# Adding the first layer's expert outputs in smaller pieces and from an earlier row, and scattering the first half's rows earlier

## The chip, the cores and the metric

The kernel runs as one program on one core of a Trainium2 chip. The metric is the device time of one execution in microseconds, as the median of several runs. The core has five engines that run side by side and meet only at semaphores: TensorE (PE), VectorE (DVE), ScalarE (ACT), GpSimd (POOL) and SyncE (SP, which here only issues transfers). TensorE's weight loads are shown apart, as PEld.

## What is computed

Two layers over 4 x 1024 tokens of width 128. `attn0` is causal attention with rotated queries and keys, `conv1` a gated convolution of length 1024 done through Fourier transforms, `moe0` a mixture of 8 experts with one expert for each token, `moe1` one with two experts for each token.

```python
x = L0_attn_x                                   # 4 x 1024 x 128
xn = layernorm(x)
x = x + attn0(xn, w_q, w_k, w_v) + moe0(xn, wg, W, b)
xn = layernorm(x)
x = x + conv1(xn, Wu, Wv, W1, W2, W3, Wo, ...) + moe1(xn, Wg, W1, b1, W2, b2)
# moe1: p = softmax(xn @ Wg); the two best experts of each token;
#       y = (relu(xs @ W1[e] + b1[e]) @ W2[e] + b2[e]) * p, added at the token
```

## The kernel before

A tile is 128 tokens; there are 32 (`NT`), 8 for each batch entry (`J`). A quarter is 8 tiles, a half (`HT`) 16. The residual stays in SBUF as `xres`, and the normalised tokens in `row`.

The order on each engine is the order in which its block of the program is written, and there are three stages that matter here.

**The attention rows.** A loop `for n in range(NT)` runs on PE, DVE and ACT alike. In its turn n, TensorE multiplies the scores of row n+1 (`scores`), transposes the probabilities of row n once ACT has exponentiated them (`transpose_probs`, L1260), and weighs the values of row n-1 (`weigh_values`). DVE takes the maximum of row n+1 (`row_max`, L1710), copies a part of the transposed probabilities (`take_pt`) and adds the attention of row n-1 to `xres` (`attention_row`, L1728). ACT exponentiates row n+1 (`exp_rows`, L1008), which waits for that maximum. The scores of row n are n % 8 + 1 tiles wide, so that rows 24 to 27 are short and 28 to 31 long.

Into these turns other work is put by tables of turn numbers. `ADD_AT` (23, 24, 26) says in which turns DVE adds a quarter of the first layer's expert outputs (`add_experts`, L1744, then `tile_stats`, L1748, and `tile_aggr`, L1752); the fourth quarter follows in turns 28, 31 and behind the loop. The outputs are read back from memory (`moe0`) into the buffer `y0`, a quarter at a time, by SP (L731), and each load but the first waits until DVE has used the quarter before. POOL then computes the reciprocal deviations (`inverse_std`, L795 and L797). `NORM_AT` says when ACT normalises the first three quarters (L1025), `GATES_AT` (26, 27, 30) when TensorE transposes them and multiplies with the gate weights of the second layer, and ACT copies the logits to `lg`. `ROUTING_AT` spreads the 30 steps of the first half's routing (`routing1`, on DVE, L1510 to L1581) over turns 28, 29 and 30; `COUNTS_AT` (29) is the turn in which TensorE counts tokens for it.

**The prelude of the second layer.** POOL scatters the rows of the first half to the experts' slots in memory, one indirect transfer for each tile and each of the two chosen experts (`dispatch`, L810), 32 in all; behind every second one it waits until the transfers have been issued. It starts when `slot1_ready` says that the routing is done. TensorE meanwhile projects the tokens (`project_vu`, 16 units), transposes the last quarter, multiplies its gates and counts; DVE does the first radix passes (L622 and after) and the second half's routing; then TensorE does 8 Fourier products (`forward`), each followed by `product` on DVE (L1822 to L1827). The list is in `conv_at(PRELUDE)`. Behind the 32, POOL scatters 8 (`SCATTER_IN_PRELUDE`) of the second half's 32.

**The expert rounds.** There are 40 rounds, each for two tiles of slots. SP loads the slots (L710) once all 32 scatters of the first half have landed (`wait_sent1(0)`); TensorE transposes them (`expert_rows`, L1414) and multiplies twice, ACT copies the experts' weights into `ring` and takes the hidden layer, DVE adds a bias (`expert1_out`, L1873), POOL sends the rows back (`send_back`, L833). Convolution work for the second layer is spread over the same rounds, and two more of the second half's scatters follow in each round. `ring` is idle between the last tiles of the first layer's experts and the copies of the second layer's weights.

## Time and profile before

| | us |
|---|---|
| median of 3 runs | 510.49 (509.75 to 511.93) |
| the profiled execution, its own time | 510.97 |
| its span, first to last instruction | 509.2 |

| engine | busy us | share of the span |
|---|---|---|
| TensorE (PE) | 373.4 | 73% |
| PE weight loads | 305.5 | 60% |
| DVE | 294.5 | 58% |
| POOL | 256.7 | 50% |
| ACT | 225.5 | 44% |

The mean granted clock of TensorE over the span is 0.914 of full speed. A row of a timeline gives the start, the length, the engine, the line, the operation, what it writes and reads, how many instructions it groups, and in brackets how long the engine had been idle before it and which event ended that. No engine is busy all the time, so the busy shares alone do not say what bounds the kernel; the stretches and the waits at their ends do.

### The profile page before, as it was taken

To read this page: it belongs to the slowest core of one execution; us is meant where nothing else is said; L and a number is where in the kernel's file an instruction comes from. 1 tells how busy PE (TensorE), PEld (TensorE's weight loads), DVE (VectorE), ACT (ScalarE), POOL (GpSimd) and SP (SyncE) were. 2 spreads that over 40 slices of the span, in tenths; PEclk is the share of its full clock that TensorE was granted. 3 is DMA by queue.
4 is the path that set the end of the run, shared out by engine and by line. 5 is a ranking of instruction groups with operands and counts; after the bars stand their busy time and mean duration, and the time that the engine had idled before them with its cause. 6 is when DMAs were issued, how large, how long until landed. Compare 5 with 4: busy or idle time off the path is not lost.

```text
span 509.2 us, 7804 instructions
## 1 busy us (share of the span) xinstructions
PE 373.4 (73%) x2302; PEld 305.5 (60%) x2302; DVE 294.5 (58%) x782; ACT 225.5 (44%) x551; POOL 256.7 (50%) x254
## 2 busy tenths in 40 slices
PE   2483689979997954977997468888887777776630
PEld 0371255956784643757996357777776766766520
DVE  4968479216755776175769953367746773244115
ACT  1472042433342326252341036533557667578824
POOL 2746766615666013003766666666666445446540
PEclk9999699979998995696998859999999999999985
DMA  9999993632311112000113263444421213622407
GB/s 221 401 230 241 173 157 87 213 92 64 91 54 43 42 42 84 0 0 12 38 38 97 69 175 119 136 121 140 119 58 56 73 32 85 195 67 77 124 14 246
DMA packets 64745, 55.05 MB, mean 108 GB/s; under 512 B 6820, under 2 KB 56684, under 8 KB 64447
## 3 DMA queue, kind: packets, MB, share of 16 engines
q1 hardware_dynamic: 57888, 41.71, 33.0%
q0 software_dynamic: 6656, 12.51, 7.8%
q10 hardware_dynamic: 158, 0.33, 0.4%
q8 instruction: 19, 0.31, 0.3%
q14 instruction: 24, 0.19, 0.1%
HBM read 30.44 MB, written 25.27 MB: 109 GB/s over the span
## 4 chain that ended last, share of the span: by engine, by line
PE 39%; issue 16%; DMA 14%; ACT 12%; POOL 11%; DVE 7%; POOLq 1%; SPq 0%; ACTq 0%; DVEq 0%
PE psO L1158 15%; PE psS L1158 14%; PE psT L1158 7%; ACT hT L1120 7%; DMA slots<-row,slot 7%; POOL slots L823 4%; POOL slots L810 3%; POOL w L844 2%; DMA moe<-ys,xs 2%; DMA xres<-in_x 2%; PE psT L1260 2%; ACT row L1025 1%; POOL moe L833 1%; DVE xres L1744 1%; DVE work L1710 1%
## 5 line engine op out<-in xcount | busy, mean ns | idle before, releaser
L833 POOL DMA_INDIRECT moe<-ys,xs x61 | 62.8, 1029 | 61.4 <-DVE ys L1873 23.4
L810 POOL DMA_INDIRECT slots<-row,slot x64 | 67.1, 1048 | 35.7 <-DMA slots<-row,slot 12.3
L1158 PE MATMUL psO<-ring,hT 128*128 128x128 f32 x320 | 46.1, 288 | 44.2 <-ACT hT L1120 44.2
L1158 PEld LDWEIGHTS psO<-ring,hT 128*128 128x128 f32 x320 | 39.5, 194 | 52.6 <-issue 52.6
L1873 DVE TENSOR_TENSOR ys<-psO,ring 128x256 f32<-128x256 f32 x40 | 16.9, 424 | 85.9 <-PE psO L1158 85.7
L1120 ACT ACTIVATE hT<-psT,ring 128x128 f32<-128x128 f32 x160 | 45.6, 368 | 46.0 <-PE psT L1158 45.8
L1053 ACT ACTIVATE ring<-w 128x642 f32 x80 | 55.7, 761 | 0.9 <-issue 0.8
L1158 PE MATMUL psS<-work 128*128 128x512 f32 (+3 forms) x96 | 41.4, 545 | 12.3 <-DVE work L1693 8.8
L833 POOL DMA_INDIRECT moe<-ys,w x35 | 37.1, 1060 | 23.8 <-DVE ys L1873 9.7
L1018 ACT ACTIVATE work<-psT 128x512 f32<-128x512 f32 (+3 forms) x32 | 16.5, 517 | 66.2 <-PE psT L1260 66.2
L823 POOL DMA_INDIRECT slots<-row,slot x32 | 34.7, 1085 | 18.2 <-DMA slots<-row,slot 10.9
L1158 PE MATMUL psT<-xsT,ring 128*128 128x128 f32 x320 | 43.3, 279 | 0.5 <-ACT xsT L1113 0.5
L1158 PEld LDWEIGHTS psT<-xsT,ring 128*128 128x128 f32 x320 | 40.7, 195 | 1.4 <-ACT xsT L1113 0.8
L1158 PE MATMUL psO<-work 128*128 128x128 f32 x288 | 41.3, 294 | 0.0
L1008 ACT ACTIVATE work<-psS,work 128x128 f32<-128x128 f32 (+7 forms) x32 | 23.6, 739 | 38.9 <-DVE work L1714 38.8
L1710 DVE TENSOR_REDUCE work<-psS 128x1 f32<-128x128 f32 (+7 forms) x32 | 24.0, 749 | 26.0 <-PE psS L1158 24.5
L1158 PEld LDWEIGHTS psO<-work 128*128 128x128 f32 x288 | 38.8, 211 | 0.0
L795 POOL TENSOR_SCALAR veps<-mv 128x8 f32<-128x8 f32 (+1 forms) x9 | 2.4, 265 | 68.4 <-DVE slot L1577 32.6
L1260 PE MATMUL psT<-cst,work 128*128 128x128 f32 x144 | 24.6, 304 | 13.8 <-ACT work L1008 13.8
L1158 PEld LDWEIGHTS psS<-work 128*128 128x128 f32 x96 | 18.0, 214 | 27.0 <-issue 18.6
L1158 PE MATMUL psS<-work,mats 128*128 128x256 f32 x128 | 32.0, 411 | 2.9 <-DVE work L673 2.6
L1158 PE MATMUL psS<-xT,work 128*128 128x512 f32 x64 | 30.9, 625 | 1.3 <-ACT work L1008 1.3
(271 smaller groups left out, 801.1 us busy)
## 6 DMA issues: line engine op xcount, KB each, us to landing
slots<-xs SPq DMA_DIRECT2D x14, 516.0 KB, 12.7
mats<-in_iv SPq DMA_DIRECT2D x16, 256.0 KB, 3.4
xs<-slots SPq DMA_DIRECT2D x61, 64.5 KB, 1.9
w<-in_w SPq DMA_DIRECT2D x8, 321.0 KB
w<-slots SPq DMA_DIRECT2D x35, 64.5 KB, 1.9
xres<-in_x SPq DMA_DIRECT2D x4, 512.0 KB, 9.5
mats<-in_fw SPq DMA_DIRECT2D x1, 2048.0 KB, 11.1
moe<-xs SPq DMA_DIRECT2D x4, 512.0 KB, 6.9
```

Source lines behind the costliest of these rows:

```text
L810: pool.indirect_dma_start(slots1[:, :], bass.IndirectOffsetOnAxis(ap=(slot1, slot2)[k][:, i:i + 1], axis=0), row[:, i, :], None, bounds_ch ...
L823: pool.indirect_dma_start(dst[:, :], bass.IndirectOffsetOnAxis(ap=slots[:, i:i + 1], axis=0), row[:, i, :], None, bounds_check=bound, oob_ ...
L833: pool.indirect_dma_start(dst[:, :], bass.IndirectOffsetOnAxis(ap=row_slots[l][m][:, D:ROWW].bitcast(I32), axis=0), ys[:, n % UNROLL, :], ...
L844: pool.tensor_tensor(t[0:FO, :], t[0:FO, :], hx[0:FO, :], op).then_inc(f_pool, 1)
L1008: act.activation(prob[n % 2][:, 0:(i + 1) * P], S[n % 2][:, :, :].rearrange("p a m -> p (a m)")[:, 0:(i + 1) * P], ACT.Exp, bias=negmax[:, ...
L1018: act.activation(pT[n % 2][:, 0:k, :].rearrange("p j q -> p (j q)"), t_bank("p", n, 0)[:, 0:k * P], ACT.Copy).then_inc(pt_act, 1)
L1053: act.activation(pair_w[p % RING_PAIRS][:, t, :], w12[:, bass.ds(e, 1), :].rearrange("p e h -> p (e h)"), ACT.Copy).then_inc(e_w, 1)
L1120: last = act.activation(hT[:, k, :], TP[1][:, k * P:(k + 1) * P], ACT.Relu, bias=pair_w[p % RING_PAIRS][:, k // 2, B1_AT + k % 2:B1_AT + k ...
L1158: return pe.matmul(o, lhsT, rhs, start=start, stop=stop)
L1260: last = pe.transpose(t_bank("p", n, c)[:, (j - 4 * c) * P:(j - 4 * c + 1) * P], prob[n % 2][:, j * P:(j + 1) * P], ident)
L1710: dve.tensor_reduce(negmax[:, n:n + 1], S[n % 2][:, :, :].rearrange("p a m -> p (a m)")[:, 0:(n % J + 1) * P], X, ALU.max, negate=True).th ...
L1873: tt(ys[:, m:m + 2, :], O[p % 2][:, 0:2 * D].rearrange("p (t d) -> p t d", d=D), pair_w[p % RING_PAIRS][:, :, B2_AT:W_COLS], ALU.add).then ...
```

## The change

Four things are changed together.

- The loads of the expert outputs: quarters 0, 1 and 2 go to three buffers (`y0` and two parts of `ring`) and are issued one behind the other; quarter 3 waits for the use of quarter 0. Each has a semaphore of its own. ACT waits for the use of the first three before it copies weights into `ring`.
- The additions: pieces of four tiles (later two and one), each with its statistics, some before the row maximum of a turn (`ADD_BEFORE_MAX`) and some behind the row (`ADD_BEHIND_ROW`), from turn 21 on.
- Norms, gates and counts are two turns earlier or so, and the routing of the first half is in turns 26 to 28, again partly before the row maximum.
- In the prelude, the last quarter's transposes and gates come behind 5 and 8 projections, not 8 and 10; both halves of the last quarter's `inverse_std` stand inside the scatter (before dispatch 4 and 12); 12 of the second half's scatters are done ahead of the rounds, not 8; and SP loads the first inverse matrices behind slots 3, 5 and 14, not four of them ahead of all slots.

`ISSUES_APART_IN_ROUNDS` is 2, as `ISSUES_APART` is, and changes nothing.

```diff
-GATES_AT = (26, 27, 30)
-NORM_AT = {25: [(0, 0), (0, 1)], 26: [(1, 0), (1, 1)], 28: [(2, 0)], 29: [(2, 1)]}
-ROUTING_AT = {28: 12, 29: 10, 30: R1_STEPS}
-COUNTS_AT = 29
+GATES_AT = (24, 25, 29)
+NORM_AT = {23: [(0, 0), (0, 1)], 24: [(1, 0), (1, 1)], 27: [(2, 0)], 28: [(2, 1)]}
+COUNTS_AT = 27
-ADD_AT = (23, 24, 26)
+ADD_BEFORE_MAX = {22: (4, 8), 23: (12, 16), 25: (20, 24), 29: (24, 28), 31: (28, 30)}
+ADD_BEHIND_ROW = {21: (0, 4), 22: (8, 12), 24: (16, 20)}
+ROUTING_BEFORE_MAX = {26: 6, 28: 8}
+ROUTING_BEHIND_ROW = {26: 6, 27: 10, 28: R1_STEPS}
-SCATTER_IN_PRELUDE, SCATTER_PIECES = 8, 2
-NORM_IN_SCATTER = 6
+SCATTER_IN_PRELUDE, SCATTER_PIECES = 12, 2
+NORM_IN_SCATTER = (4, 12)
+FIRST_INV_MATS = {3: (0, 1), 5: (2, 3), 14: (4, 5, 6, 7)}
-        return (vu[:8] + [("t", 2 * B - 2), ("t", 2 * B - 1)] + vu[8:10] + [("g", B - 1)] + vu[10:14] + [("rc", 2)] + vu[14:]
+        return (vu[:5] + [("t", 2 * B - 2), ("t", 2 * B - 1)] + vu[5:8] + [("g", B - 1)] + vu[8:12] + [("rc", 2)] + vu[12:]
+        y0_groups = [y0, *(ring[:, n * J * D:(n + 1) * J * D].rearrange("p (j d) -> p j d", d=D) for n in range(2)), y0]
             for g in range(B):
-                if g:
-                    sp.wait_ge(y0_used, J * g)
-                sp.dma_start(y0, moe0[g * L:(g + 1) * L, :].rearrange("(j p) d -> p j d", p=P)).then_inc(y0_loaded, 16)
+                if g == B - 1:
+                    sp.wait_ge(y0_used, J)
+                sp.dma_start(y0_groups[g], moe0[g * L:(g + 1) * L, :].rearrange("(j p) d -> p j d", p=P)).then_inc(y0_loaded[g], 16)
-            for c in range(NC // 2):
-                inverse_mats(0, c)
             wait_sent1(0)
...
-                if n == RING[1] - 1:
-                    for c in range(NC // 2, NC):
+                if n in FIRST_INV_MATS:
+                    for c in FIRST_INV_MATS[n]:
                         inverse_mats(0, c)
...
-            inverse_std(2 * B - 1, 0, J // 2)
             for i in range(HT):
-                if i == NORM_IN_SCATTER:
-                    inverse_std(2 * B - 1, J // 2, J // 2)
+                if i in NORM_IN_SCATTER:
+                    inverse_std(2 * B - 1, J // 2 * NORM_IN_SCATTER.index(i), J // 2)
                 dispatch(0, 0, i)
...
+            act.wait_ge(y0_used, (B - 1) * J)
...
+            def add_tiles(first, end):
+                for stage in (add_experts, tile_stats, tile_aggr):
+                    for i in range(first, end):
+                        stage(i)
...
+                if n in ADD_BEFORE_MAX:
+                    add_tiles(*ADD_BEFORE_MAX[n])
+                take(first_routing, ROUTING_BEFORE_MAX.get(n, 0))
                 if n + 1 < NT:
                     row_max(n + 1)
```

The DVE order at turns 23 and 24 before: L1710 and L1714 are the maximum of row 24, L1767 the reciprocal sum, L1722 the copy of probabilities, L1728 the attention's addition, and the eight tiles follow.

```order
208 L1710 TENSOR_REDUCE work<-psS 128x1
209 L1714 TENSOR_SCALAR work<-work 128x1
210 L1767 RECIPROCAL work<-work 128x1
211 L1722 COPY work<-psT 128x512
212 L1728 SCALAR_TENSOR_TENSOR xres<-psO,work,xres 128x128
213 L1744 SCALAR_TENSOR_TENSOR xres<-work,gate,xres 128x128 x8
214 L1748 BN_STATS stats<-xres 128x6 x8
215 L1752 BN_AGGR mv<-stats 128x2 x8
216 L1710 TENSOR_REDUCE work<-psS 128x1
```

The DVE order now, in turns 22 and 23: L1713 is the row maximum (row 23, then row 24), L1747 the addition; the third and fourth piece read from `ring`.

```order
206 L1747 SCALAR_TENSOR_TENSOR xres<-work,gate,xres 128x128 x4
207 L1751 BN_STATS stats<-xres 128x6 x4
208 L1755 BN_AGGR mv<-stats 128x2 x4
209 L1713 TENSOR_REDUCE work<-psS 128x1
210 L1717 TENSOR_SCALAR work<-work 128x1
211 L1778 RECIPROCAL work<-work 128x1
212 L1725 COPY work<-psT 128x384
213 L1731 SCALAR_TENSOR_TENSOR xres<-psO,work,xres 128x128
214 L1747 SCALAR_TENSOR_TENSOR xres<-ring,gate,xres 128x128 x4
```

By the maximum of row 24, 16 tiles have been added where none had been.

POOL before, from the last quarter's first deviations (L795, L797) through the scatters (L810) to the first rows sent back (L833).

```order
40 L795 TENSOR_SCALAR veps<-mv 128x4
41 L797 TENSOR_TENSOR rstd<-veps,cst 128x4
42 L810 DMA slots<-row,slot 10240x129 x6
43 L795 TENSOR_SCALAR veps<-mv 128x4
44 L797 TENSOR_TENSOR rstd<-veps,cst 128x4
45 L810 DMA slots<-row,slot 10240x129 x10
46 L819 COPY row<-cst 128x8 x2
47 L810 DMA slots<-row,slot 10240x129 x24
48 L833 DMA moe<-ys,xs 8192x128 x2
```

POOL now, the same place (L813 is the scatter, L798 and L800 the deviations, L836 the sending back).

```order
40 L813 DMA slots<-row,slot 10240x129 x4
41 L798 TENSOR_SCALAR veps<-mv 128x4
42 L800 TENSOR_TENSOR rstd<-veps,cst 128x4
43 L813 DMA slots<-row,slot 10240x129 x8
44 L798 TENSOR_SCALAR veps<-mv 128x4
45 L800 TENSOR_TENSOR rstd<-veps,cst 128x4
46 L813 DMA slots<-row,slot 10240x129 x4
47 L822 COPY row<-cst 128x8 x2
48 L813 DMA slots<-row,slot 10240x129 x28
49 L836 DMA moe<-ys,xs 8192x128 x2
```

Four scatters now stand ahead of the first deviations and twelve ahead of the second; 28, not 24, stand between the relabelling (`second_ids`) and the first sending back.

SP before, from the loads of the expert outputs on.

```order
23 L731 DMA work<-moe 128x8x128 x4
24 L738 DMA mats<-in_iv 128x512 x4
25 L710 DMA xs<-slots 128x129 x8
26 L710 DMA w<-slots 128x129 x7
27 L738 DMA mats<-in_iv 128x512 x4
```

SP now.

```order
23 L736 DMA work<-moe 128x8x128
24 L736 DMA ring<-moe 128x8x128 x2
25 L736 DMA work<-moe 128x8x128
26 L715 DMA xs<-slots 128x129 x4
27 L743 DMA mats<-in_iv 128x512 x2
28 L715 DMA xs<-slots 128x129 x2
29 L743 DMA mats<-in_iv 128x512 x2
```

The first inverse matrices moved behind the first four slot loads.

## Rows read from the trace of the kernel before

**Rows 1.** Busy time of each engine in stretches: microseconds, instructions, granted clock, DMA.

```profile
core 0: us, PE busy (x) PEld busy (x) DVE busy (x) ACT busy (x) POOL busy (x), PEclk, DMA share, GB/s
168.29:243.53 75.24, 56.11 (x300) 45.34 (x301) 45.52 (x178) 27.68 (x68) 12.44 (x19) 0.80 0.10 30
243.53:270.38 26.85, 24.24 (x220) 23.33 (x217) 19.50 (x52) 12.62 (x23) 18.07 (x19) 1.00 0.11 36
270.38:286.67 16.29, 16.01 (x64) 13.12 (x64) 14.84 (x39) 0.00 (x0) 10.15 (x11) 0.90 0.38 105
286.67:296.22 9.55, 0.00 (x1) 0.01 (x1) 8.82 (x17) 0.00 (x0) 6.31 (x7) 0.61 0.21 59
296.22:311.17 14.95, 12.48 (x55) 10.66 (x56) 4.10 (x9) 8.14 (x19) 10.02 (x10) 0.68 0.66 177
```

**Rows 2.** Timeline of TensorE: prelude's start, Fourier products, first slots of the rounds.

```profile
243.53 0.22 PE L1158 MATMUL psS<-biasb,pickb 96*128 96x128 bf16 x1
...
270.38 14.04 PE L1158 MATMUL psS<-work,mats 128*128 128x256 f32 x56 [2.61 <-DVE work L673]
...
296.22 0.74 PE L1414 MATMUL psT<-cst,xs 128*128 128x128 f32 x2 [9.55 <-DMA xs<-slots]
...
297.43 2.08 PE L1158 MATMUL psT<-xsT,ring 128*128 128x128 f32 x8 [0.47 <-ACT xsT L1113]
```

**Rows 3.** Timeline of POOL's scatter and of SP's first slot loads.

```profile
235.68 0.23 POOL L795 TENSOR_SCALAR veps<-mv 128x4 f32<-128x4 f32 x1 [32.62 <-DVE slot L1577]
...
243.47 0.97 POOL L810 DMA_INDIRECT slots<-row,slot  x1 [0.78 <-DMA slots<-row,slot]
...
250.89 2.02 POOL L810 DMA_INDIRECT slots<-row,slot  x1 [0.78 <-DMA slots<-row,slot]
...
290.74 0.97 POOL L810 DMA_INDIRECT slots<-row,slot  x1 [0.30 <-issue]
...
294.00 3.66 SPq L710 DMA_DIRECT2D xs<-slots  x8
```

**Rows 4.** Timeline of DVE in the attention rows: additions, routing, last statistics.

```profile
176.43 1.22 DVE L1710 TENSOR_REDUCE work<-psS 128x1 f32<-128x1024 f32 x1
...
182.09 2.18 DVE L1744 SCALAR_TENSOR_TENSOR xres<-work,gate,xres 128x128 f32<-128x128 f32 x8
...
185.75 0.62 DVE L1752 BATCH_NORM_AGGREGATE mv<-stats 128x2 f32<-128x6 f32 x8
...
218.05 0.36 DVE L1510 TENSOR_REDUCE m<-lg 128x16 f32<-128x128 f32 x1
...
235.24 0.17 DVE L1577 CAST slot<-m 128x16 int32<-128x16 f32 x1
...
245.52 0.36 DVE L1752 BATCH_NORM_AGGREGATE mv<-stats 128x2 f32<-128x6 f32 x4
```

**Rows 5.** TensorE's waits for the exponentials, 168.3 to 243.5 us, grouped.

```profile
L1260 PE MATMUL psT<-cst,work 128*128 128x128 f32 x57 | 10.6, 330 | 10.6 <-ACT work L1008 10.6
```

**Rows 6.** Timeline: ACT's norms of one quarter, and the first gates on TensorE.

```profile
193.74 3.17 ACT L1025 ACTIVATE row<-xres,veps,rstd 128x128 f32<-128x128 f32 x8
...
201.65 3.55 PE L1158 MATMUL psO<-wg,xT 128*128 128x8 f32 x16 [3.20 <-ACT xT L1030]
```

**Rows 7.** SP's first load of expert outputs, and the four from issue to landing.

```profile
166.02 0.37 SPq L731 DMA_DIRECT2D work<-moe  x1
...
work<-moe SPq DMA_DIRECT2D x4, 512.0 KB, 3.9
```

**Rows 8.** Timeline of DVE: second routing's wait, the first three rounds' outputs.

```profile
259.97 0.37 DVE L1510 TENSOR_REDUCE m<-lg 128x16 f32<-128x128 f32 x1 [4.16 <-ACT lg L1034]
...
302.91 0.42 DVE L1873 TENSOR_TENSOR ys<-psO,ring 128x256 f32<-128x256 f32 x1 [5.61 <-PE psO L1158]
...
311.20 0.42 DVE L1873 TENSOR_TENSOR ys<-psO,ring 128x256 f32<-128x256 f32 x1 [5.28 <-PE psO L1158]
...
318.00 0.42 DVE L1873 TENSOR_TENSOR ys<-psO,ring 128x256 f32<-128x256 f32 x1 [3.37 <-PE psO L1158]
```

More of the change, by code:

```diff
@@ L228 @@
 ISSUES_APART = 2
+ISSUES_APART_IN_ROUNDS = 2
 def conv_at(r):
@@ L491, in two_layer_kernel @@
         e_ha = sem("e_ha")
-        y0_loaded = sem("y0_loaded")
+        y0_loaded = [sem(f"y0_loaded{g}") for g in range(B)]
         y0_used = sem("y0_used")
@@ L799, in _, with after_issue @@
             n_issued = [0]
-            def after_issue():
+            def after_issue(apart=ISSUES_APART):
                 n_issued[0] += 1
-                if n_issued[0] % ISSUES_APART == 0:
+                if n_issued[0] % apart == 0:
                     pool.wait_ge(issued, n_issued[0])
@@ L836, in send_back @@
                     engine_sem=issued).then_inc(sent_back[m], 16)
-                after_issue()
+                after_issue(ISSUES_APART_IN_ROUNDS if l else ISSUES_APART)
             n_pool = [0]
@@ L1741, in add_experts @@
                 g, j = divmod(i, J)
[L1742 removed]
+                dve.wait_ge(y0_loaded[g], 16)
                 dve.wait_ge(o_done, i + 1)
[L1744 removed]
+                stt(xres[:, i, :], y0_groups[g][:, j, :], gate0[:, i:i + 1], xres[:, i, :], ALU.mult, ALU.add).then_inc(y0_used, 1)
             def tile_stats(i):
@@ L1780, in _ @@
                     expert0_bias(e)
-                if n in ADD_AT:
-                    g = ADD_AT.index(n)
-                    for stage in (add_experts, tile_stats, tile_aggr):
-                        for i in range(J * g, J * g + J):
-                            stage(i)
-                if n in ROUTING_AT:
-                    take(first_routing, ROUTING_AT[n])
-                if n == NT - 4:
-                    for stage in (add_experts, tile_stats):
-                        for i in range(NT - 8, NT - 4):
-                            stage(i)
-                if n == NT - 3:
-                    for i in range(NT - 8, NT - 4):
-                        tile_aggr(i)
+                if n in ADD_BEHIND_ROW:
+                    add_tiles(*ADD_BEHIND_ROW[n])
+                take(first_routing, ROUTING_BEHIND_ROW.get(n, 0))
                 if n == NT - 1:
                     norm_rows(2 * B - 1, 0, J // 2)
-                    for i in range(NT - 4, NT - 1):
-                        add_experts(i)
+                    add_tiles(NT - 2, NT - 1)
             attention_row(NT - 1)
-            add_experts(NT - 1)
-            for stage in (tile_stats, tile_aggr):
-                for i in range(NT - 4, NT):
-                    stage(i)
+            add_tiles(NT - 1, NT)
             norm_rows(2 * B - 1, J // 2, J // 2)
```

4 lines of the change are left out of this document (1 added, 3 removed).

## The prediction

> **What bounds the kernel now.** I read the stretches first [rows 1], then TensorE's waits [rows 2, 5], then the engines that end them. The rounds start only when TensorE has the first slots: it finishes its Fourier products at 286.67 and stands still for 9.55 us, until the loads that SP issued at 294.00 land [rows 2, 3]. Those loads wait for POOL's 32 scatters. POOL begins at 235.68, at once when DVE has written the slot numbers, and the last of the 32 is issued at 290.74 [rows 3]. So the chain before the rounds is: routing done on DVE, then 294.00 - 235.68 = 58.32 us of scatter, then 2.22 us of load. Beside it runs a second chain that is 9.55 us shorter: attention rows end at 243.53, 26.85 us of projections, 16.29 us of Fourier products [rows 1, 2]. From the rounds on nothing of the order changes much, so whatever the start gains, the end gains; the reader should see that two chains have to be shortened together, and that the shorter one caps the gain.
>
> The stage that feeds both is the attention rows from turn 21 on: 75.24 us with TensorE busy for 56.11 at a clock of 0.80 [rows 1]. Of its 19.1 us idle, 10.6 are waits for an exponential [rows 5], and those wait for a row maximum that stands behind added work in DVE's queue.
>
> **The additions (turns 21 to 25).** The sum over eight tiles was 182.09 to 186.37, 4.28 us [rows 4], so a piece of four is about 2.1 us. Nothing is added or removed in all: about 17 us of DVE work moves to other places, and DVE is busy for only 45.5 of the 75.2 us [rows 1]. The first load is issued at 166.02 and lands 3.9 us later, at 169.9 [rows 7], in time for turn 21 at about 171. The next two go into other buffers; even one behind the other at 3.9 us each they land by 177.8, before their use at about 181 and 189. A cost lies in turns 21 and 22: two pieces, 4.3 us, stand ahead of the maximum of row 23, which was at 176.43 [rows 4]; about 1.6 us of it fill time in which DVE waited for the projections there, so the maximum comes at about 179.1, and TensorE loses 2.7 us. After that the same work is no longer in turns 23 and 24. By my hand schedule, with these lengths and the waits of each engine's order: 16 tiles are added by 186, where before eight had been at 186.37, and the second eight followed at about 192.5. I take 6.5 us sooner for the second quarter.
>
> **Norms, gates and routing.** ACT needs 3.17 us for a quarter, and the first gates take 3.55 us at the low clock [rows 6]. From 186 on: deviations, about 2.7 us; the first quarter's norms are done at about 190.5, the second's at 194.6; the first gates run from 195 to 199, row 26's scores and the second transposes follow, and the second gates' logits are there at about 205.4. Routing's first step was at 218.05 and slots were written at 235.41 [rows 4], 17.4 us for 28 steps with row work between. Now its first 6 steps stand before the maximum of row 27, and wait for those logits: 205.4. The 28 steps are some 10 us of DVE; between them stand three row maxima and their small work (4 us) and ACT's exponential. I get the slots at about 219.5. The bounds are 218 (no low clock in the gates) and 226 (every wait before a maximum costs TensorE a full round trip again). So POOL starts 16.2 us sooner (9.7 to 17.7).
>
> TensorE pays for it: it stands idle while the maximum of row 29 waits behind 8 steps of routing, about 5 us, where it now idles before rows 30 and 31. The end of the rows comes from that: with the clock of before I get 242, with full clock 239, and no gain at all is 243.53. I take 242, 1.5 us sooner, since the gaps are as many as before and the clock of 0.80 is the nearest row.
>
> **The scatter.** It starts at 219.5. Its 58.32 us hold both pairs of deviations, and so they do now. New is a wait before dispatch 12: POOL gets there some 20 us after its start, at 240, but the last tile's statistics come about 1.3 us behind the rows' end (2.35 us before, for four tiles [rows 4]), at 243.3, so 3 us are lost. Slots are loaded from 219.5 + 58.3 + 3 = 280.8, and TensorE has them at 283.0.
>
> A scatter instruction takes 0.97 us, but 2.02 at 250.89, where DVE runs its 128x1024 additions; the one at 243.47, under the expert additions, takes 0.97 [rows 3]. Of the Trainium skill, "SBUF — State Buffer", section "SBUF: two separate sides", speaks against this change here: DVE instructions with two SBUF inputs and GpSimd instructions that read SBUF shut each other out for a whole instruction. By it, the 12 scatters that now run beside the rows' additions could each be held up for one of them, 0.28 us; the row at 243.47 doesn't show it. I leave it at nothing in the sum; by the rule, the first slots would come at up to 286.4.
>
> **The prelude.** The last quarter's gates stand two projections earlier, and DVE waited 4.16 us for them [rows 8]. Of 26.85 us for 16 projections and the rest, one is some 1.35 us, so the second routing starts 2.7 us sooner and the Fourier products too; TensorE waited 2.61 us for that radix pass [rows 2], which bounds this gain. TensorE is done at 242 + 24.1 + 16.3 = 282.4. Both chains thus meet at 282 to 283. The 12 scatters, 4 more than before, put 6 us ahead of the first sending back; DVE needs the buffers of rounds 0 and 1 only four rounds later, 27 us, which hides them. The matrices that SP loads behind slots 3 and 5 are needed two hand-offs later and were loaded early before; at most 1 us.
>
> **The clock.** TensorE enters the rounds at a clock of 0.61 to 0.68 after its 9.55 us of idleness [rows 1]; its first 8 multiplications take 2.08 us, and the first two outputs are 8.29 us apart, the next two 6.80 [rows 8]. With an idle time under 1 us that penalty mostly goes: 1.5 us for the first round, about 1 us for each of two groups of eight. I take 3 us; the ends are 0 and 4.
>
> **The sum.** 296.22 - 283.0 = 13.2 us, and 3 for the clock: 16.2. The profiled execution's 510.97 becomes 494.8; the median of the runs is 0.5 below it, so I say 495.0 for both.
>
> **Rivals.**
> 1. *The routing comes late.* DVE's queue waits for the second quarter's logits before the maximum of row 27, and so TensorE, ACT and DVE take turns. For it: three engines' hand-offs lie between norms and logits. Slots at 226 give first slots at 289.5, a gain of 6.7 and some 2 of clock: 502 (499 to 505).
> 2. *DVE bounds the first rounds.* Its products end some 18 us behind the routing, at about 290.5, and three radix pieces stand ahead of the first output, which so comes at 294 and not at 289. Against it: rounds need that output only two rounds later. If it stops ACT's third weight copy, 3 us are lost: 498.
> 3. *The rows gain more.* Rows end at 239, POOL starts at 218, and the clock is full: first slots at 279.5 to 281, 4 of clock: 487 to 491.
> 4. *Slower.* The pieces before a maximum each hold up exponential, transposes and the next scores, five of them 2.1 us and two of routing 2 to 2.6, some 15 us in all, and none is paid back by the waits that go. It decides once the rows end more than 12.3 us later (9.55 of slack and 2.7 of the prelude), at 256 or more, which also delays the last quarter's norms inside POOL's queue: 511 to 517, say 514. Against it: DVE's work there is the same as before and it idles 30 us.
>
> **Chances.** The forecast (491 to 499) 0.52; rival 1 0.20; rival 2 0.07; rival 3 0.11; slower 0.07; within 0.5% (the parts cancel) 0.03. 0.5%, 2.6 us, is about what a measurement of this kernel can tell from no change. The range 489 to 503 leaves out rival 4, no change, and the far ends of rivals 1 and 3, 0.19 in all. Faster: 0.90.
>
> **What would show it.** Right: POOL's scatter starts at 218 to 221; the maximum of row 23 is 2 to 3 us late; TensorE's wait before the first slots falls from 9.55 us to under 2; the clock of the first round is above 0.9, and its outputs are 6.8 us apart; the rounds after it last as long as before. Wrong: the first scatter at 226 or later; an idle time of over 4 us at the first slots (the scatter alone bounds); a wait of DVE for sent rows in round 4 (the 12 scatters cost something); rows ending later than 246.

## The result, and the profile of the changed kernel

The changed kernel takes **492.23 us** (median of 4 runs, 491.0 to 493.85); the kernel before took 510.73 in the runs beside it. The ratio is 0.9639, with an interval of 0.9600 to 0.9677: faster by 3.6%. The profiled execution took 493.04, its span 491.2, at a mean granted clock of 0.934 (0.914 before). The forecast of 495.0 was 2.8 us too high.

In short: POOL's scatter starts 17 us sooner and the step in it that wants the last tile holds it up for only 2.9 us, the attention rows end 5 us sooner, so the first slots are transposed 15 us sooner; another 3 us come from a TensorE that no longer enters the rounds at its low clock.

The times inside the changed kernel's trace are read with one correction. Upstream of anything that the change touches its timeline is already about 1.0 us late (the maximum of row 22 stands at 169.25, before at 168.29 in [rows 1]), so a milestone that moved by x gained about x + 1. That lateness is a difference between executions: in a second trace of the same kernel (changed_again) the maximum of row 22 stands at 166.64. The third output and the span are compared as they stand.

First the stretches, at the same events as [rows 1] (columns as there: length of the stretch, busy time and instructions of each engine, granted clock, DMA); the last two lines divide the rounds at the second output.

```profile
169.25:238.19 68.94, 52.57 (x300) 41.12 (x301) 46.15 (x183) 27.98 (x68) 20.40 (x26) 0.85 0.14 40
238.19:265.57 27.38, 24.25 (x220) 23.35 (x218) 21.73 (x57) 10.62 (x20) 16.86 (x17) 1.00 0.09 30
265.57:281.08 15.51, 15.51 (x67) 13.30 (x65) 13.57 (x32) 2.08 (x3) 9.70 (x11) 0.89 0.19 51
281.08:293.11 12.03, 8.64 (x56) 7.54 (x55) 11.26 (x23) 8.06 (x19) 8.49 (x7) 1.00 0.95 276
293.11:318.00 24.89, 21.58 (x128) 19.10 (x126) 11.05 (x22) 11.94 (x29) 15.96 (x18) 1.00 0.36 106
```

Read the first number behind the colon pairs against [rows 1]: rows 75.24 to 68.94, prelude 26.85 to 27.38, Fourier products 16.29 to 15.51, and the stretch of 9.55 us in which TensorE waited for slots is not there at all. The first slots come at 281.08 and not at 296.22.

TensorE's timeline has the same events (start, length, engine, line, operation, how many, and in brackets the idle time ahead and what ended it), and two waits that matter.

```profile
220.91 1.54 PE L1263 MATMUL psT<-cst,work 128*128 128x128 f32 x6 [6.54 <-ACT work L1010]
...
227.73 3.33 PE L1161 MATMUL psS<-work 128*128 128x512 f32 x4
...
238.19 0.22 PE L1161 MATMUL psS<-biasb,pickb 96*128 96x128 bf16 x1
...
264.23 0.23 PE L1161 MATMUL psS<-biasb,pickb 96*128 96x128 bf16 x1 [3.13 <-DVE tables L1530]
...
265.57 15.67 PE L1161 MATMUL psS<-work,mats 128*128 128x256 f32 x64
281.08 0.40 PE L1417 MATMUL psT<-cst,xs 128*128 128x128 f32 x2
281.95 1.16 PE L1161 MATMUL psT<-xsT,ring 128*128 128x128 f32 x8 [0.47 <-ACT xsT L1115]
```

Against [rows 2]: the brackets at the first slots are gone, and the first eight multiplications take 1.16 us where they took 2.08. The wait of 2.61 us before the Fourier products is gone too, but one of 3.13 us ends 1.3 us ahead of them: TensorE wants to write a bank of PSUM that DVE's routing (L1530) has not read yet.

POOL and SP, to set against [rows 3]:

```profile
218.78 1.12 POOL L813 DMA_INDIRECT slots<-row,slot  x1 [22.37 <-DVE slot L1580]
220.20 0.97 POOL L813 DMA_INDIRECT slots<-row,slot  x1 [0.30 <-issue]
...
240.27 0.23 POOL L798 TENSOR_SCALAR veps<-mv 128x4 f32<-128x4 f32 x1 [2.87 <-DVE mv L1755]
...
260.63 2.52 POOL L813 DMA_INDIRECT slots<-row,slot  x1 [0.89 <-DMA slots<-row,slot]
```

```profile
278.53 1.80 SPq L715 DMA_DIRECT2D xs<-slots  x4
```

The scatter starts at 218.78, waits 2.87 us for the last statistics before dispatch 12, and lets SP load at 278.53, 15.5 us sooner than the 294.00 of before. With 2.2 us to land that is 280.7: the slots are there just before TensorE is. Both chains now meet, and TensorE's is the last by a few tenths of a microsecond.

DVE, to set against [rows 4] and [rows 8]:

```profile
179.60 1.19 DVE L1713 TENSOR_REDUCE work<-psS 128x1 f32<-128x1024 f32 x1
...
185.59 0.36 DVE L1755 BATCH_NORM_AGGREGATE mv<-stats 128x2 f32<-128x6 f32 x4
...
204.08 0.37 DVE L1513 TENSOR_REDUCE m<-lg 128x16 f32<-128x128 f32 x1 [3.50 <-ACT lg L1036]
...
217.71 0.17 DVE L1580 CAST slot<-m 128x16 int32<-128x16 f32 x1
...
289.89 0.42 DVE L1868 TENSOR_TENSOR ys<-psO,ring 128x256 f32<-128x256 f32 x1
293.11 0.42 DVE L1868 TENSOR_TENSOR ys<-psO,ring 128x256 f32<-128x256 f32 x1 [0.25 <-PE psO L1161]
299.91 0.42 DVE L1868 TENSOR_TENSOR ys<-psO,ring 128x256 f32<-128x256 f32 x1 [3.37 <-PE psO L1161]
```

The maximum of row 23 is 3.2 us later than the 176.43 of before (2.2 with the correction), the 16th tile's statistics are there at 185.95, the routing begins 14 us sooner and the slot numbers are written 17.5 us sooner. The third output is 18.1 us sooner (318.00 to 299.91) and the span 18.0 us shorter (509.2 to 491.2): nothing behind the third output changed.

### The profile page after: what moved, and what is told of

Read it like the earlier page. It is cut to its first block, busy times and chain, and to the rows that moved or that the text cites. A ratio compares the mean times of both kernels' runs of the same rounds, so it can differ in the third digit from the quotient of the medians.

```text
span 491.2 us, 7805 instructions
## 1 busy us (share of the span) xinstructions
PE 366.0 (75%) x2302; PEld 298.7 (61%) x2302; DVE 294.4 (60%) x782; ACT 225.9 (46%) x551; POOL 258.4 (53%) x254
## 4 chain that ended last, share of the span: by engine, by line
PE 44%; issue 13%; ACT 12%; DVE 10%; DMA 10%; POOL 8%; SPq 1%; ACTq 0%; POOLq 0%; DVEq 0%
PE psS L1161 19%; PE psO L1161 15%; PE psT L1161 7%; ACT hT L1122 7%; POOL slots L826 4%; DMA slots<-row,slot 4%; DMA moe<-ys,xs 2%; POOL w L847 2%; DMA xres<-in_x 2%; ACT row L1027 1%; PE psT L1263 1%; POOL moe L836 1%; DVE work L1713 1%; DVE xres L1747 1%; DMA moe<-ys,ring 1%
## 5 line engine op out<-in xcount | busy, mean ns | idle before, releaser
L813 POOL DMA_INDIRECT slots<-row,slot x64 | 69.3, 1083 | 57.0 <-DVE slot L1580 22.4
L836 POOL DMA_INDIRECT moe<-ys,xs x61 | 61.1, 1001 | 58.3 <-issue 16.6
L1161 PE MATMUL psS<-work 128*128 128x512 f32 (+3 forms) x96 | 42.6, 558 | 12.6 <-DVE work L1696 8.8
L836 POOL DMA_INDIRECT moe<-ys,w x35 | 38.0, 1087 | 23.3 <-DVE ys L1868 9.7
L826 POOL DMA_INDIRECT slots<-row,slot x32 | 34.9, 1091 | 18.1 <-DMA slots<-row,slot 10.9
L1161 PE MATMUL psT<-xsT,ring 128*128 128x128 f32 x320 | 42.3, 275 | 0.5 <-ACT xsT L1115 0.5
L1161 PE MATMUL psO<-work 128*128 128x128 f32 x288 | 39.7, 286 | 0.0
L1713 DVE TENSOR_REDUCE work<-psS 128x1 f32<-128x128 f32 (+7 forms) x32 | 24.0, 750 | 25.5 <-PE psS L1161 23.9
L1161 PEld LDWEIGHTS psO<-work 128*128 128x128 f32 x288 | 37.1, 203 | 0.0
L1161 PEld LDWEIGHTS psS<-work 128*128 128x128 f32 x96 | 17.9, 214 | 27.5 <-issue 18.5
L1263 PEld LDWEIGHTS psT<-cst,work 128*128 128x128 f32 x144 | 17.0, 153 | 23.2 <-ACT work L1010 18.3
L1161 PE MATMUL psS<-work,mats 128*128 128x256 f32 x128 | 30.1, 395 | 0.0
```

The lines of the kernel that those rows point to most:

```text
L813: pool.indirect_dma_start(slots1[:, :], bass.IndirectOffsetOnAxis(ap=(slot1, slot2)[k][:, i:i + 1], axis=0), row[:, i, :], None, bounds_ch ...
L826: pool.indirect_dma_start(dst[:, :], bass.IndirectOffsetOnAxis(ap=slots[:, i:i + 1], axis=0), row[:, i, :], None, bounds_check=bound, oob_ ...
L836: pool.indirect_dma_start(dst[:, :], bass.IndirectOffsetOnAxis(ap=row_slots[l][m][:, D:ROWW].bitcast(I32), axis=0), ys[:, n % UNROLL, :], ...
L1161: return pe.matmul(o, lhsT, rhs, start=start, stop=stop)
L1263: last = pe.transpose(t_bank("p", n, c)[:, (j - 4 * c) * P:(j - 4 * c + 1) * P], prob[n % 2][:, j * P:(j + 1) * P], ident)
L1713: dve.tensor_reduce(negmax[:, n:n + 1], S[n % 2][:, :, :].rearrange("p a m -> p (a m)")[:, 0:(n % J + 1) * P], X, ALU.max, negate=True).th ...
```

## Experiments

Each kernel ran beside the kernel before on its own chip. Medians are compared through those runs; milestones are from the traces. "The changed kernel with ..." names what is edited in it.

**One part undone.** Four kernels ran together (the kernel before beside them: 512.1).

The order of the prelude as before:

```diff
-        return (vu[:5] + [("t", 2 * B - 2), ("t", 2 * B - 1)] + vu[5:8] + [("g", B - 1)] + vu[8:12] + [("rc", 2)] + vu[12:]
+        return (vu[:8] + [("t", 2 * B - 2), ("t", 2 * B - 1)] + vu[8:10] + [("g", B - 1)] + vu[10:14] + [("rc", 2)] + vu[14:]
```

> The changed kernel, with only the order of the prelude put back (8 projections ahead of the last quarter's transposes, 10 ahead of its gates, 14 ahead of the counts). Theory of the prediction (the earlier gates bring the Fourier products 2.7 us sooner, and these lead to the first round): 2.7 us longer than the changed kernel, near 495. Rival, from the trace of the changed kernel: there TensorE waits 3.13 us for routing results in the bank of the counts, which took the gain back, so this kernel starts its Fourier products 0 to 0.5 us apart from the changed one and takes the same time, within 0.7 us; DVE's products end some 2 us later, which the first two rounds hide.

493.71 us, ratio 0.9662 (0.9618 to 0.9707). TensorE's timeline:

```profile
264.56 14.12 PE L1161 MATMUL psS<-work,mats 128*128 128x256 f32 x56 [2.59 <-DVE work L678]
```

The rows end at 237.72, so the Fourier products start 26.84 us behind them, as before the change (26.85), and with the change they start 27.38 us behind. The gates really come sooner, but the counts also do: they stand behind 12 projections, not 14, hold a PSUM bank until DVE has reached L1530, and a projection that rotates onto that bank waits for it. One wait was exchanged for another. By the ratios this kernel is 1.2 us longer than the changed one, which the intervals don't tell apart; the 2.7 us of the theory are not there.

The deviations of the last quarter where they were, the first before all scatters, the second before dispatch 6:

```diff
-NORM_IN_SCATTER = (4, 12)
+NORM_IN_SCATTER = 6
...
+            inverse_std(2 * B - 1, 0, J // 2)
             for i in range(HT):
-                if i in NORM_IN_SCATTER:
-                    inverse_std(2 * B - 1, J // 2 * NORM_IN_SCATTER.index(i), J // 2)
+                if i == NORM_IN_SCATTER:
+                    inverse_std(2 * B - 1, J // 2, J // 2)
```

> The changed kernel, with only the places of the last quarter's deviations in POOL's scatter put back (first pair ahead of all scatters, second behind 6). Theory (the scatter chain leads to the first round, and the places keep POOL from waiting for the end of the attention rows): the scatter starts at 223.8 and not 218.8, six scatters are done by the wait for the last tile at 240 where it was twelve, so the first slots come 9 us later and the kernel takes 500 to 502. Rival (Fourier products lead, the scatter has slack): under 3 us longer.

505.0 us, ratio 0.9878 (0.9834 to 0.9922). POOL's two deviations, and TensorE's first slots:

```profile
223.90 0.23 POOL L798 TENSOR_SCALAR veps<-mv 128x4 f32<-128x4 f32 x1 [28.32 <-DVE mv L1756]
...
241.41 0.23 POOL L798 TENSOR_SCALAR veps<-mv 128x4 f32<-128x4 f32 x1 [7.49 <-DVE mv L1756]
```

```profile
290.90 0.47 PE L1418 MATMUL psT<-cst,xs 128*128 128x128 f32 x1 [8.49 <-DMA xs<-slots]
```

With the slot numbers there at 219.07, about as in the changed kernel, POOL stands 4.8 us before its first scatter, since the first pair of deviations wants tiles 24 to 27, and 7.49 us before its seventh, since the second wants the last tile. SP loads at 289.14, 10.6 us later; TensorE's idle time comes back, and with it the low clock (0.50 from 290.90 to 298.38), so that the third output stands 22.53 us behind the first slots and not 18.83. The expectation of 500 to 502 had left that out. The third output is 13.5 us later (313.43), but some 2 us of it aren't the edit's: this execution was the longest of its four, its second gates took 3.56 us and not 1.92, and its rows end 2.0 us later behind the maximum of row 23. By the ratios of the runs (0.9878 and 0.9639) this one edit carries some 12 of the 18.5 us.

It can do so only together with the rows. In the kernel before there is no such wait to take away; POOL stands there for 0.35 us:

```profile
246.07 0.23 POOL L795 TENSOR_SCALAR veps<-mv 128x4 f32<-128x4 f32 x1 [0.35 <-DVE mv L1752]
```

No run has the new places without the new rows.

The loads into one buffer, one behind the use of the other:

```diff
-        y0_groups = [y0, *(ring[:, n * J * D:(n + 1) * J * D].rearrange("p (j d) -> p j d", d=D) for n in range(2)), y0]
+        y0_groups = [y0, y0, y0, y0]
...
-                if g == B - 1:
-                    sp.wait_ge(y0_used, J)
+                if g:
+                    sp.wait_ge(y0_used, J * g)
```

> The changed kernel with one buffer for the expert outputs, each load behind the use of the quarter before. Theory: the pieces leave time for a load of 3.9 us, DVE waits some 0.9 us in turn 22 and 0.5 us in turn 24, routing and rows come about 1 us later: 492 to 494. Rival (three loads at once are what lets the additions start in turn 21): 4 us or more longer, 496 and up.

494.22 us, ratio 0.9669 (0.9635 to 0.9702); third output at 300.33, 0.4 us later; by the ratios 1.5 us longer, with intervals that overlap. The early pieces hardly need the three buffers: a load of 3.9 us finds its place between two quarters.

8 scatters in the prelude and the inverse matrices first:

```diff
-SCATTER_IN_PRELUDE, SCATTER_PIECES = 12, 2
+SCATTER_IN_PRELUDE, SCATTER_PIECES = 8, 2
-FIRST_INV_MATS = {3: (0, 1), 5: (2, 3), 14: (4, 5, 6, 7)}
+FIRST_INV_MATS = {14: (4, 5, 6, 7)}
...
+            for c in range(NC // 2):
+                inverse_mats(0, c)
             wait_sent1(0)
```

> The changed kernel with 8 scatters of the second half ahead of the rounds and the first four inverse matrices loaded ahead of all slots. Theory: both are hidden before and after, 491.5 to 493, the same as the changed kernel. Rival (12 scatters shorten the rounds, or the matrices delayed the first inverse products): over 1.5 us apart.

495.41 us, ratio 0.9696 (0.9653 to 0.9740); third output at 300.73. POOL sends the first rows back at 290.80, not at 299.32, and it brings nothing, since DVE needs the buffers only rounds later. The third output is 0.8 us later than in the changed kernel: the first slots come 0.9 us sooner (280.18), and the first round, where this execution had a low clock, gives up 1.7 (eight output products 2.05 us, 1.13 in the changed kernel). The expectation of 491.5 to 493 was missed. By the ratios this kernel is 2.9 us longer, with intervals that overlap, and the trace is that of its shortest execution. So whether the two edits are worth anything is open.

**One part alone**, and two questions on waits (the kernel before beside them: 510.51). The attention rows, loads and routing of the change, with the prelude's order, the deviations, the 8 scatters and the matrices of before:

```diff
-SCATTER_IN_PRELUDE, SCATTER_PIECES = 12, 2
-NORM_IN_SCATTER = (4, 12)
-FIRST_INV_MATS = {3: (0, 1), 5: (2, 3), 14: (4, 5, 6, 7)}
+SCATTER_IN_PRELUDE, SCATTER_PIECES = 8, 2
+NORM_IN_SCATTER = 6
+FIRST_INV_MATS = {14: (4, 5, 6, 7)}
...
-        return (vu[:5] + [("t", 2 * B - 2), ("t", 2 * B - 1)] + vu[5:8] + [("g", B - 1)] + vu[8:12] + [("rc", 2)] + vu[12:]
+        return (vu[:8] + [("t", 2 * B - 2), ("t", 2 * B - 1)] + vu[8:10] + [("g", B - 1)] + vu[10:14] + [("rc", 2)] + vu[14:]
```

> The kernel before with only the attention rows changed (additions in pieces, three loads, earlier norms, gates and routing); prelude order, deviations' places, 8 scatters and matrices as before. Theory (scatter chain, which loses 9 us to the old places of the deviations): 500 to 502, about half of the gain. Rival (the rows bring the gain, the rest is small): 493 to 495.

504.3 us, ratio 0.9873 (0.9825 to 0.9921), 2 to 4 us more than expected, and again the low clock had been left out (first slots to third output 21.85 us, 18.83 in the changed kernel). The rows end as early as in the changed kernel (237.25), and the gain stays unused:

```profile
289.78 1.09 PE L1420 MATMUL psT<-cst,xs 128*128 128x128 f32 x2 [9.40 <-DMA xs<-slots]
```

Rows alone bring 6.2 us. No run has the rows and the places of the deviations alone; that these two bring most of the 18.5 follows from undo_norm_places and from the runs with another part undone, which lose 1.2 to 2.9 us each by the ratios.

The kernel before with the prelude's order, the 12 scatters and the matrices of the change:

```diff
-SCATTER_IN_PRELUDE, SCATTER_PIECES = 8, 2
+SCATTER_IN_PRELUDE, SCATTER_PIECES = 12, 2
+FIRST_INV_MATS = {3: (0, 1), 5: (2, 3), 14: (4, 5, 6, 7)}
...
-        return (vu[:8] + [("t", 2 * B - 2), ("t", 2 * B - 1)] + vu[8:10] + [("g", B - 1)] + vu[10:14] + [("rc", 2)] + vu[14:]
+        return (vu[:5] + [("t", 2 * B - 2), ("t", 2 * B - 1)] + vu[5:8] + [("g", B - 1)] + vu[8:12] + [("rc", 2)] + vu[12:]
```

> The kernel before with only the prelude's order, 12 scatters and the matrices' places changed. Theory: the Fourier products were 9.55 us ahead of the first slots, so nothing that moves them counts: 510 to 511.5. Rival (the parts add up, 2.7 us of the prelude): 508.

511.38 us, ratio 1.0007 (0.9980 to 1.0033): nothing, with the same 3.13 us of wait for L1526 and one of 8.11 before the first slots. The second would have hidden a gain as well as a loss, so this run shows the wait for the bank and not the worth of the order.

The kernel before, with TensorE kept busy while it waits for the first slots, by 150 small multiplications whose result nothing uses:

```diff
+                if r + 2 == 0:
+                    for _ in range(150):
+                        mm(TP[1][:, 0:P], identb[:, :], onesb[:, :])
                 if 0 <= r + 2 < PAIRS1:
                     expert_rows(r + 2)
```

> The kernel before with 150 small multiplications of TensorE into an unused bank between the Fourier products and the first slots, about 8 us of work in a wait of 9.55 us; their result is used by nothing. Theory (the idle time lowers the clock for the first round, 3 us): first slots at the same time, the first two outputs of DVE 6.8 and not 8.3 us apart, 507 to 508.5. Rival (the low clock in the first round costs nothing on the chain, or has another cause than idleness): 510 to 511.

508.61 us, ratio 0.9958 (0.9930 to 0.9986). TensorE's timeline:

```profile
287.54 8.54 PE L1158 MATMUL psT<-onesb,identb 128*128 128x128 bf16 x150
297.05 0.69 PE L1414 MATMUL psT<-cst,xs 128*128 128x128 f32 x2 [0.97 <-DMA xs<-slots]
298.21 1.16 PE L1158 MATMUL psT<-xsT,ring 128*128 128x128 f32 x8 [0.47 <-ACT xsT L1113]
```

The slots come no sooner, yet the first eight multiplications take 1.16 us and not 2.08, and the outputs stand at 302.40, 309.20 and 316.00: 6.80 apart, not 8.29 and 6.80 as in [rows 8]. That isolates the clock's part: 1.9 us by the medians, 2.8 by the traces (first slots to third output 18.95 us, 21.78 before). So about 2 to 3 us of the gain come from TensorE not standing still before the rounds, whatever ends its wait. The Trainium skill, "TensorE: Matmul & The Clock Gate", section "HAM oscillation — how this bites in real kernels", tells of idle time that puts the array back to its lower clock, the time being lost afterwards; this pair of runs agrees.

All of the third part of the routing behind row 28 instead of 8 steps ahead of the maximum of row 29:

```diff
-ROUTING_BEFORE_MAX = {26: 6, 28: 8}
+ROUTING_BEFORE_MAX = {26: 6}
```

> The changed kernel with the last 8 routing steps behind the row of turn 28 and not ahead of the maximum of row 29. TensorE's wait of 6.54 us there shrinks by 2.6, so the rows end that much sooner; the scatter starts 1.8 us later. Theory A (the scatter waits for the end of the rows before dispatch 12, so the rows' end leads and not its start): 1 to 2 us shorter than the changed kernel, 490 to 491.5. Theory B (the start of the scatter leads): 1.8 us longer, 494.

496.09 us, ratio 0.9703 (0.9651 to 0.9755). TensorE's wait before row 29's transposes halves, and another opens:

```profile
219.10 1.26 PE L1263 MATMUL psT<-cst,work 128*128 128x128 f32 x6 [3.38 <-ACT work L1010]
...
225.49 0.66 PE L1281 MATMUL psT<-cst,row 128*128 128x128 f32 x4 [2.33 <-DVE work L1725]
```

I had expected the rows to end 2.6 us sooner; they end at 240.68, 2.5 later, and the scatter starts 2.8 later. The steps stand in DVE's queue ahead of the maximum of row 30 instead, and the 3.16 us that the first wait lost come back as 2.33 in the other. The rest of the lateness isn't the edit's: the routing's first step, which comes before it, is already 1.0 us late (205.08), and the second and third gates took 3.56 us each and not 1.92. So this place was no better, and by how much it is worse is not shown.

**Towards a better version** (the kernel before beside the first three: 509.75, beside the last: 511.25). The changed kernel once more, for a reference on the same chip:

> The changed kernel itself, once more, as the measure for the kernels beside it on the same chip: 491 to 494.

492.22 us, ratio 0.9659 (0.9621 to 0.9697); the same rows as in the first trace, among them the 3.13 us and a wait of POOL of 2.80. One row is new: though the maximum of row 22 is 2.6 us sooner here (166.64), that of row 23 is only 1.1 sooner (178.51), because DVE waits 1.42 us for the first load of expert outputs before its first addition (170.71). The additions now begin so early that the load can hold them up, which it could not before the change.

The last deviations before dispatch 14, and the counts behind 14 projections, where the bank is no longer in the way:

```diff
-NORM_IN_SCATTER = (4, 12)
+NORM_IN_SCATTER = (4, 14)
-vu[8:12] + [("rc", 2)] + vu[12:]
+vu[8:14] + [("rc", 2)] + vu[14:]
```

> The changed kernel with the last tile's deviations before dispatch 14 and not 12, and the second half's counts behind 14 projections and not 12. Theory (three chains end together at the first slots: the scatter with its wait of 2.87 us at dispatch 12, the Fourier products with TensorE's wait of 3.13 us for the counts' bank, and neither alone can give more than the other): both waits go, TensorE has the first slots 2.5 us sooner, DVE's products end 0.6 us sooner, 2 to 2.6 us shorter than the changed kernel. Rival (DVE's products and radix pieces ahead of the first output lead by now): 0.6 us shorter at most.

491.93 us, ratio 0.9641 (0.9597 to 0.9684): no gain that can be told. Both waits are gone, and the first slots come 40.5 us behind the rows' end, not 42.9; but the third output only 60.8 behind it, not 61.7. The scatter is no longer what leads: SP loads at 273.91, 4.3 us ahead of TensorE's first slots (278.25). TensorE then runs at a low clock in the first round, in this stretch and these two groups:

```profile
282.00:289.00 7.00, 6.85 (x31) 6.21 (x32) 6.69 (x12) 2.70 (x6) 4.84 (x5) 0.76 0.97 273
...
282.15 1.95 PE L1161 MATMUL psO<-ring,hT 128*128 128x128 f32 x8 [1.66 <-issue]
283.89 4.50 PE L1161 MATMUL psS<-work,mats 128*128 128x256 f32 x16
```

The two groups take 1.13 and 3.62 us in the changed kernel; the 1.7 us between are about what the first round lost (20.33 us from the first slots to the third output, 18.83 in the changed kernel). The rival, that DVE's products lead by now, doesn't explain it: busy_before_row_29 below has the same prelude and the same work on DVE, and there it is 18.66. Why the clock fell is open. TensorE had stood still for 1.66 us just before, but it does so at the same place in the changed kernel too (1.81 us), and there the clock held.

The same counts with the deviations of the changed kernel, 50 multiplications that nothing uses before the first gates, and 100 before row 28's transposes:

```diff
-vu[8:12] + [("rc", 2)] + vu[12:]
+vu[8:14] + [("rc", 2)] + vu[14:]
+                    if g == 0:
+                        for _ in range(50):
+                            mm(o_bank("g", g)[:, 0:P], identb[:, :], onesb[:, :])
...
+                if n == 28:
+                    wait_emptied(pe, T_USES, T_AT[("p", n, 0)])
+                    for _ in range(100):
+                        mm(t_bank("p", n, 0)[:, 0:P], identb[:, :], onesb[:, :])
```

> The changed kernel with the counts behind 14 projections, and 50 small unused multiplications of TensorE in its wait before the first gates (3.4 us) and 100 in its wait of turn 28 (6.5 us). Theory (the clock falls in those waits, and the slow multiplications behind them stand on the chain): gates take 1.9 and not 3.55 us, scores of row 31 1.9 and not 3.3, the rows end 3 us sooner, POOL no longer waits at dispatch 12; first slots 4 to 5 us sooner, 487 to 489. Rival (the slow multiplications lie beside waits for other engines): within 1 us of the changed kernel.

491.23 us, ratio 0.9622 (0.9586 to 0.9659). The expectation of 487 to 489 was missed. The profiled execution was the longest of its six (495.5), so its third output (302.15) says little. The first gates take 1.92 us and not 3.55, and with both traces lined up at their start the routing's first step is 2.0 us sooner, but the rows' end only 0.7, as the third gates took 3.22 us here and not 1.92. POOL waits 4.26 us before dispatch 12 and TensorE 2.04 us for the slots, so with the deviations there the scatter leads again. And I had put the 100 one row too early: the 6.54 us of wait are before row 29's transposes. So the last run has them there, and the deviations before dispatch 14:

```diff
-NORM_IN_SCATTER = (4, 12)
+NORM_IN_SCATTER = (4, 14)
-                if n == 28:
+                if n == 29:
```

> The changed kernel with four edits: the last norm before dispatch 14 instead of 12, the counts behind 14 projections instead of 12, 50 multiplications whose result nothing uses ahead of the first gates, and 100 of them ahead of row 29's transposes, in the 6.55 us in which TensorE waits for that exponential. Theory that the clock falls after that wait and that this sets the rows' end: gates(0) at 1.9 us, the scores behind row 29's transposes at about 1.95 us instead of 3.3, the gates of the third quarter at 1.9, rows' end 2 us sooner (235.1 to 236 on the changed kernel's timeline of 237.1 to 238.2), Fourier products start 25.5 us behind it, first scatter about 1.5 us sooner, no wait of POOL for the last statistics; third output at 296 to 297 instead of 298.8 to 299.9; median 488.5 to 490. Rival, that the row maxima and exponentials and not TensorE's clock set the rows' end: fillers take as long as the wait at most, rows end within 0.5 us of before, third output at 298 to 299.5, median 491 to 492.5. The 100 take 5.8 us at full clock, more at the low one: should they end behind the exponential, the rows are up to 3 us later, median 493 to 495.

**489.55 us** (487.42 to 493.49, 6 runs), ratio 0.9602 (0.9557 to 0.9647), the lowest of all; the interval overlaps that of the changed kernel (0.9600 to 0.9677), so by the ratios some 1.9 to 2.9 us, 0.4 to 0.6%, are likely and not certain. Its profiled execution (487.60, span 485.8) is one of its shortest. Stretches of that trace, the rows, the prelude and the Fourier products, then a piece of the rows:

```profile
168.20:235.58 67.38, 58.11 (x458) 45.59 (x457) 47.45 (x188) 28.58 (x68) 20.46 (x26) 0.95 0.16 43
235.58:259.79 24.21, 24.21 (x221) 23.33 (x218) 18.90 (x46) 10.63 (x20) 15.64 (x17) 1.00 0.11 37
259.79:275.72 15.93, 15.05 (x65) 11.80 (x65) 14.48 (x39) 1.99 (x3) 10.12 (x11) 1.00 0.22 60
...
225.20:228.50 3.30, 3.30 (x8) 1.32 (x8) 0.00 (x0) 0.28 (x1) 2.07 (x3) 0.59 0.12 40
```

```profile
191.30 2.96 PE L1161 MATMUL psO<-onesb,identb 128*128 128x128 bf16 x50
194.91 1.92 PE L1161 MATMUL psO<-wg,xT 128*128 128x8 f32 x16 [0.66 <-ACT xT L1032]
...
212.19 5.75 PE L1161 MATMUL psT<-onesb,identb 128*128 128x128 bf16 x100
218.90 0.87 PE L1267 MATMUL psT<-cst,work 128*128 128x128 f32 x6 [0.96 <-ACT work L1010]
```

```profile
294.38 0.43 DVE L1875 TENSOR_TENSOR ys<-psO,ring 128x256 f32<-128x256 f32 x1 [1.62 <-PE psO L1161]
```

Set against the changed kernel with both lined up at the start of the first gates (194.20 there, 194.91 here, so 0.71 late): the routing's first step is 2.8 us sooner (204.08 to 202.03), row 29's transposes 2.7 (220.91 to 218.90), the last scores 3.2 (227.73 to 225.23), the rows' end 3.3 (238.19 to 235.58). So in this trace the 50 multiplications, which cover a wait of 3.44 us, bring 2.8 us, and the 100, which cover 6.54, bring 0.5; no run has one of them without other edits, and in kept_busy_and_counts the 50 brought 2.0. The expectation had it the other way round: it priced the scores behind row 29 at 1.95 us, and they take 3.2 at a clock of 0.59 although TensorE had been busy before them. The prelude is 24.21 us, 3.2 shorter, with no wait, and this time the clock of the first round held; the first slots are at 275.72, 40.1 us behind the rows' end. The Fourier products take 15.93 us at full clock, where the changed kernel needed 15.51 at 0.89: TensorE now waits 0.3 us for DVE's product before each of the last three, so in this stretch DVE begins to set the pace.

## Why the prediction was right, by its own steps

- **What bounds the kernel**: right. Two chains lead to the first slots, both had to be shortened, and the cap of the shorter one held: with the scatter's chain left long (undo_norm_places, rows_alone) TensorE idles 8.5 to 9.4 us there.
- **The additions**: right in this trace, though the first load came just in time (see changed_again). Maximum of row 23 expected at 179.1, measured 179.60; 16 tiles by 186, measured 185.95; TensorE's loss there was put at 2.7 us; its wait before that row's transposes grew from 0.98 to 2.61 us, and they start 3.1 us later, 2.2 with the correction.
- **Norms, gates, routing**: right within 2 us. Second logits 205.4 (204.08), slot numbers 219.5 (217.88). Rival 1, a routing at 226, did not happen: the hand-offs cost what the hand schedule said.
- **The rows' end**: too small. The step "I take 242, 1.5 us sooner, since the gaps are as many as before and the clock of 0.80 is the nearest row" failed. The rows end at 238.19, 5.3 us sooner (6.3 with the correction), just beyond the bound of 239. By the stretches, TensorE's busy time fell by 3.5 us (56.11 to 52.57, the clock going from 0.80 to 0.85) and its idle time by 2.8 (19.1 to 16.4), together 6.3. I had counted the gaps, not their sum, and had held the clock fixed. Which of the smaller gaps raised it is not shown.
- **The scatter**: right. Start 219.5 (218.78), wait for the last statistics 3 (2.87), loads issued 280.8 (278.53); of these 2.3 us the start gives 0.7 and the scatter itself 1.4, as it took 56.9 us without its wait and not 58.3. The rule of the Trainium skill on the port that DVE and GpSimd share was left out of the sum, and rightly: all 12 scatters that run beside the rows took 0.96 to 1.12 us (the row at 220.20, beside an addition of four tiles, 0.97). The one of 2.52 us at 260.63 ran beside three 128x512 operations of DVE with two operands in SBUF and the short ones behind them, the one of 2.02 us of before [rows 3] beside a 128x1024 one. But one at 245.20, beside another 128x1024 operation, took 1.24 us. So the Trainium skill's rule ("SBUF — State Buffer", "SBUF: two separate sides") may be seen at long instructions, though not at each; for 128x128 additions the trace doesn't show it.
- **The prelude**: half wrong. Of "the second routing starts 2.7 us sooner and the Fourier products too" the first half came true (251.96 is 13.77 us behind the rows' end, before 16.44), and the second failed: the products start 0.5 us later behind the rows' end than before. The sum looked at the wait that goes (2.61 us) and not at what the counts, moved with the gates, keep occupied: a PSUM bank that a projection wants, 3.13 us. undo_prelude_order shows no worth of the edit that its runs can tell, and later_norm_and_counts and busy_before_row_29 that with the counts two projections later the prelude has no wait.
- **The first slots**: expected 283.0, measured 281.08. On TensorE's chain the sum closes: rows 5.3 sooner, prelude 0.5 later, Fourier 0.8 sooner, wait 9.55 gone, together 15.1. The two wrong terms, 3.8 too little and 3.2 too much, nearly cancelled, and TensorE's chain, forecast at 282.4, ended last, not the scatter's (283.0). That the forecast came so near owes something to luck: had only the prelude's term been wrong, TensorE's chain would have ended at 282.4 + 3.2 = 285.6.
- **The clock**: 3 us expected, 2.95 measured (18.09 at the third output less 15.14 at the first slots), and its mechanism shown by busy_while_waiting (2.8 by its trace, 1.9 by its runs).
- **Rival 2** (DVE bounds the first rounds) did not happen: DVE takes the first output at 289.89, some 3.6 us after TensorE has made it, but TensorE and ACT never wait for DVE there, and from the second output on DVE waits for TensorE again; **rival 3** had the right size for the rows and the wrong one for the whole, since the prelude took back what it gave. **The rounds** were untouched, as said: no wait of DVE for sent rows, and undo_twelve_and_mats has the same spacing with four scatters fewer.

## What to carry to other kernels

When two chains meet at one point, price the change on both and look for what couples them: here a queue's small step (two instructions that want the last tile) held some 12 of 18.5 us, because it stood ahead of work that needed nothing of it, and it cost nothing as long as the tile was ready. When a producer is moved earlier, ask which buffer or bank it now holds longer and which later instruction rotates onto it. Idle time of TensorE can cost more than its length, so sum the idle time of a stretch, not its gaps. Where a wait can't be removed, multiplications that nothing uses can pay for themselves: 150 did before the rounds; 50 seem to have done so before the gates, which others wait for, and 100 hardly did before row 29.

## What the runs showed of the hardware

- 9.55 us of idle time before the rounds cost about 2 to 3 us after it: eight multiplications 2.08 us instead of 1.16, two outputs 8.29 us apart instead of 6.80. Filled with 150 multiplications, the same wait cost none of this, and the program was 1.9 us shorter.
- The clock also falls where TensorE had no long wait: 0.59 in the scores at 225.20 of busy_before_row_29, though TensorE had been busy for 5.05 of the 6.30 us before them, at full clock; 0.76 in the first round of later_norm_and_counts, and a slow group of output products in undo_twelve_and_mats, both behind a wait of about 1.65 us that in busy_before_row_29 had no such effect. No run here settles the cause.
- A pair of POOL's scatters takes about 3.03 us at the least in the changed kernel (229.09 to 232.12: two instructions of 0.97, 0.30 between them, 0.78 of wait for transfers) and mostly under 3.4; the longest took 4.68 (260.63 to 265.31). Sixteen pairs at 3.03 are 48.5 us, so it is mostly their number that sets the 58 us; the rest is the deviations, the relabelling and the pairs that took longer.
